# Reordering a software-pipelined two-layer graph attention kernel on TensorE: transposes of the next pair ahead of the scores, softmax rows transposed as a padded block, another order in prologue and drain

## What is computed

```python
def L0(X, adj, mask, Wqk, Wv):             # a softmax over the nodes
    q, k = split(X @ Wqk); v = X @ Wv
    agg = einsum('bij,bjd->bid', adj, k * mask)
    w = (1 / 16) * mask * einsum('bid,bid->bi', q, agg)
    return softmax(w, axis=1)[:, :, None] * v

def L1(x, adj, Wq, bq, Wk, bk, Wv, bv):    # dense attention, weighted by adj
    q, k, v = x @ Wq.T + bq, x @ Wk.T + bk, x @ Wv.T + bv
    weight = adj * exp(einsum('bqd,bkd->bqk', q, k))
    weight = weight / sum(weight, axis=2)
    return einsum('bqk,bkd->bqd', weight, v)

x = layernorm(x + L0(x, adj, ...)); x = layernorm(x + L1(x, adj, ...))
```

## Time and profile before

| | us |
|---|---|
| median of 3 runs | 321.32 |
| lowest, highest | 320.49, 321.69 |
| the profiled execution | 320.88 |
| its span, first to last instruction | 319.0 |
| TensorE busy | 303.7 (95%) |
| TensorE weight loads busy | 271.3 (85%) |
| VectorE busy | 221.3 (69%) |
| ScalarE busy | 200.4 (63%) |
| GpSimd busy | 141.7 (44%) |
| mean granted clock of TensorE | 0.993 of full |

### The profile page before, as it was taken

How to read it: one execution, slowest core, us unless ns; L and a number is a source line. 1 busy time by engine, 2 the same in 40 slices (tenths; PEclk the granted TensorE clock), 3 DMA queues, 4 the chain that set the end, 5 groups by cost and what they waited for, 6 DMA issues and landing times. The chain is left out here.

```text
span 319.0 us, 6523 instructions
## 1 busy us (share of the span) xinstructions
PE 303.7 (95%) x1898; PEld 271.3 (85%) x1898; DVE 221.3 (69%) x689; ACT 200.4 (63%) x456; POOL 141.7 (44%) x177
## 2 busy tenths in 40 slices
PE   8979999999999999999999999999999999999770
PEld 6758898889998988899989888999898889998660
DVE  1476777777767787777777877777778777767652
ACT  3445556667666666676666666766666667665562
POOL 1355553334555544345555344455553344553312
PEclk9999999999999999999999999999999999999997
DMA  7820223222333332323333332223333322110002
GB/s 247 296 66 36 82 85 115 86 82 84 100 115 115 115 114 83 82 87 94 115 115 115 115 87 78 83 98 115 115 115 115 91 73 82 66 53 34 33 35 99
DMA packets 19021, 31.26 MB, mean 98 GB/s; under 512 B 2112, under 2 KB 6336, under 8 KB 19008
## 3 DMA queue, kind: packets, MB, share of 16 engines
q1 hardware_dynamic: 19008, 31.11, 31.0%
HBM read 22.71 MB, written 8.39 MB: 97 GB/s over the span
## 5 line engine op out<-in xcount | busy, mean ns | idle before, releaser
L258 POOL TENSOR_TENSOR rstd<-var_eps,minus_half 128x4 f32<-128x4 f32 x35 | 35.6, 1017 | 157.6 <-ACT x L315 86.0
L315 ACT ACTIVATE x<-x_sum,shift,rstd 128x256 f32<-128x256 f32 x64 | 35.0, 594 | 48.6 <-POOL shift L261 48.6
L522 PE MATMUL ps<-w_hi,xt_hi 128*128 128x512 f32 x128 | 61.6, 482 | 0.4 <-DVE w_lo L511 0.3
L524 PE MATMUL ps<-w_hi,xt_lo 128*128 128x512 f32 x128 | 50.3, 393 | 0.0
L523 PE MATMUL ps<-w_lo,xt_hi 128*128 128x512 f32 x128 | 50.2, 392 | 0.0
L282 POOL TENSOR_TENSOR x1b<-x,bv_all 128x512 f32<-128x512 f32 x32 | 41.3, 1289 | 2.4 <-ACT x L315 2.4
L266 POOL TENSOR_TENSOR xt_lo<-xt_raw,xt_hi 128x512 fp32r<-128x512 f32 x31 | 40.0, 1290 | 4.8 <-ACT xt_hi L309 4.8
L522 PE MATMUL ps<-wv_hi,x1t_hi 128*128 128x258 f32 x128 | 38.9, 304 | 0.0
L362 ACT ACTIVATE z<-ps,z_bias 128x256 f32<-128x256 f32 x64 | 26.8, 470 | 16.3 <-PE ps L524 16.3
L315 ACT ACTIVATE x<-x,shift,rstd 128x256 f32<-128x256 f32 x64 | 34.9, 594 | 3.2 <-POOL shift L261 3.2
L394 DVE CUSTOM_DVE_ANT_0 agg<-ps,agg,adjt 128x256 f32<-128x256 f32 x64 | 31.0, 484 | 8.3 <-issue 5.7
(11 more groups left out here) (77 smaller groups left out, 646.0 us busy)
## 6 DMA issues: line engine op xcount, KB each, us to landing
xt_raw<-xt_pairs SPq DMA_DIRECT2D x32, 256.0 KB, 2.8
x_raw<-x_pairs SPq DMA_DIRECT2D x32, 256.0 KB, 2.7
out_pairs<-x SPq DMA_DIRECT2D x32, 256.0 KB, 2.0
adjt<-adjt_pairs SPq DMA_DIRECT2D x32, 129.0 KB, 2.1
p<-params SPq DMA_DIRECT2D x1, 770.0 KB, 6.8
p<-params SPq DMA_DIRECT2D x1, 512.0 KB, 3.8
p<-params SPq DMA_DIRECT2D x1, 256.0 KB, 4.8
bv_all<-value_bias SPq DMA_DIRECT2D x1, 128.0 KB, 7.5
```

Source lines behind the costliest of these rows:

```text
L258: nc.gpsimd.tensor_tensor(rstd[r % 2][:, :, :], var_eps[:, :, :], minus_half[:, :, :], ALU.pow)\
L315: last = nc.scalar.activation(out[:, graph(g)], in_[:, graph(g)], ACT.Identity, bias=shift[r % 2][:, layer, g:g + 1], scale=rstd[r % 2][:, ...
L522: nc.tensor.matmul(out, s_hi, m_hi, start=first, stop=False)
L524: return nc.tensor.matmul(out, s_lo, m_hi, start=False, stop=last)
```

## The change

- The x1 transposes become `transpose_x1(u, r)` and stand for pair t+1 between the values and the scores of slot t, instead of for pair t at the head of slot t. The copy `x1t` gets two buffers, and ScalarE makes it ahead of the exponentials.
- `p_row` becomes 128x128, zero but for its first two rows, and is transposed as a whole block.
- Prologue: the warm-up reads the zeroed `p_row`, has eight products and does not wait for `ident`; the second half of `m0` is split last; the projection of pair 0 is cut in halves with the aggregation after the first; pair 2 is masked, and aggregated, ahead of slot 0; `wv_lo` moves from slot -2 to slot -1 on GpSimd.
- Drain: in slot 30 ScalarE makes z before the norm of x1 of pair 31; in slot 31 TensorE does z before attend, and VectorE splits x1t first; the last output norm is made by VectorE in two halves, from `neg_mean` and `rstd`, and each half has its own store.

The diff, cut to its core:

```diff
...
-WARM_UP = 7
+WARM_UP = 8
...
-p_row = sb("p_row", [2, 128])
+p_row = sb("p_row", [128, 128])
...
-x1t = sb("x1t", [128, HALVES, 2, 128])
+x1t = [sb(f"x1t{i}", [128, HALVES, 2, 128]) for i in range(2)]
...
+p_row_zeroed = sem("p_row_zeroed")
...
-x1_done, out_done = sem("x1_done"), sem("out_done")
+x1_done, out_done, last_out_done = sem("x1_done"), sem("out_done"), sem("last_out_done")
...
 def w_row_ps(r):
...
+def p_full_ps(r):
+    return yv_ps(r)[:, 1, 0:NODES]
 def p_col_ps(r):
-    return yv_ps(r)[:, 1, 0:2]
+    return p_full_ps(r)[:, 0:2]
...
 def norms(t):
...
-        if exists(t - 3):
+        if r == LAST:
+            for g in range(2):
+                sp.wait_ge(last_out_done, g + 1)
+                sp.dma_start(out_pairs[t - 3][:, graph(g)], x2[(r - 3) % 4][:, graph(g)])\
+                    .then_inc(out_stored[(r - 3) % 4], 16)
+        elif exists(t - 3):
...
-    for q in out_stored:
-        sp.wait_ge(q, 16 + 16 * PAIRS // 4)
+    for n, q in enumerate(out_stored):
+        sp.wait_ge(q, 16 + 16 * PAIRS // 4 + 16 * (n == (PAIRS - 1) % 4))
...
 def _(pool):
...
-            mask_adj(t + 3, r + 3)
+            mask_adj(1, 1)
+            mask_adj(2, 2)
+        if r == -1:
...
-        if exists(t + 3) and r != -2:
+        if exists(t + 3) and r >= 0:
...
+    nc.gpsimd.memset(p_row[:, :], 0.0).then_inc(p_row_zeroed, 1)
...
+    def bias_z(t, r):
+        act.wait_ge(z_done, t + 1)
+        if r == 0:
+            act.wait_ge(biases_ready, 1)
+        for m in range(HALVES):
+            last = nc.scalar.activation(z[:, m, :], z_ps[:, m, :], ACT.Identity, bias=z_bias[:, m:m + 1])
+        last.then_inc(z_copied, 1)
     def slot(t, r):
+        if exists(t):
+            act.wait_ge(x1t_done, t + 1)
+            if exists(t - 2):
+                act.wait_ge(score_done, t - 1)
+            nc.scalar.copy(x1t[r % 2][:, :, :, :], x1t_ps).then_inc(x1t_copied, 1)
...
-        if exists(t):
-            act.wait_ge(x1t_done, t + 1)
-            nc.scalar.copy(x1t[:, :, :, :], x1t_ps).then_inc(x1t_copied, 1)
...
-        if exists(t - 3):
+        if exists(t - 3) and r != LAST:
...
+        if r == PAIRS - 2:
+            bias_z(t, r)
...
-        if exists(t):
-            act.wait_ge(z_done, t + 1)
-            if r == 0:
-                act.wait_ge(biases_ready, 1)
-            for m in range(HALVES):
-                last = nc.scalar.activation(z[:, m, :], z_ps[:, m, :], ACT.Identity, bias=z_bias[:, m:m + 1])
-            last.then_inc(z_copied, 1)
+        if exists(t) and r != PAIRS - 2:
+            bias_z(t, r)
...
+    act.wait_ge(m0_done, 1)
+    nc.scalar.activation(w0_hi[:, 0, 0:DIM], m0_ps[:, 0, :], ACT.Copy, scale=ATT_SCALE).then_inc(m0_hi_done, 1)
+    act.wait_ge(wv0_loaded, 16)
...
-        act.wait_ge(m0_done, m + 1)
-        nc.scalar.activation(w0_hi[:, m, 0:DIM], m0_ps[:, m, :], ACT.Copy, scale=ATT_SCALE).then_inc(m0_hi_done, 1)
-        act.wait_ge(wv0_loaded, 16)
...
+    act.wait_ge(m0_done, HALVES)
+    nc.scalar.activation(w0_hi[:, 1, 0:DIM], m0_ps[:, 1, :], ACT.Copy, scale=ATT_SCALE).then_inc(m0_hi_done, 1)
...
-    def split_x1t(t):
+    def split_x1t(t, r):
...
-        nc.vector.tensor_copy(x1t_hi[:, :, :, :], x1t[:, :, :, :]).then_inc(x1t_hi_done, 1)
+        nc.vector.tensor_copy(x1t_hi[:, :, :, :], x1t[r % 2][:, :, :, :]).then_inc(x1t_hi_done, 1)
...
-        nc.vector.tensor_tensor(x1t_lo[:, :, :, :], x1t[:, :, :, :], x1t_hi[:, :, :, :].bitcast(F32),
+        nc.vector.tensor_tensor(x1t_lo[:, :, :, :], x1t[r % 2][:, :, :, :], x1t_hi[:, :, :, :].bitcast(F32),
...
     def slot(t, r):
-        if r == 0:
-            split_x1t(t)
+        if r in (0, PAIRS - 1):
+            split_x1t(t, r)
...
-        if exists(t) and r != 0:
-            split_x1t(t)
+        if exists(t) and r not in (0, PAIRS - 1):
+            split_x1t(t, r)
...
-            nc.vector.tensor_scalar(p_row[:, :], exp_row[:, :], inv_sum[:, 0:1], None, ALU.mult)\
+            nc.vector.tensor_scalar(p_row[0:2, :], exp_row[:, :], inv_sum[:, 0:1], None, ALU.mult)\
...
+        if r == LAST:
+            dve.wait_ge(rstd_done, norms(t) - 1)
+            for g in range(2):
+                c = x2[(r - 3) % 4][:, graph(g)]
+                nc.vector.tensor_scalar(c, c, neg_mean[:, 1, g:g + 1], rstd[(r - 1) % 2][:, 1, g:g + 1],
+                                        ALU.add, ALU.mult).then_inc(last_out_done, 1)
...
-    for m in range(HALVES):
+    def low_m0(m):
...
+    low_m0(0)
+    for m in range(HALVES):
...
+    low_m0(1)
...
+    dve.wait_ge(consts_ready, 1)
...
+    def project_half(u, r, g, k):
+        if r == 0:
+            pe.wait_ge(m0_lo_done, k + 1)
+            pe.wait_ge(wv0_lo_done, k + 1)
+        return split_half(yv_ps(r)[:, g, :], xt_hi[r % 2][:, k, g, :], xt_lo[r % 2][:, k, g, :],
+                          w0_hi[:, k, :], w0_lo[:, k, :], k == 0, k == HALVES - 1)
     def project(u, r, g):
...
-        if r == 0:
-            pe.wait_ge(first_xt_lo_done, 1)
-        elif g == 0:
+        if g == 0:
...
-            if r == 0:
-                pe.wait_ge(m0_lo_done, k + 1)
-                pe.wait_ge(wv0_lo_done, k + 1)
-            mm = split_half(yv_ps(r)[:, g, :], xt_hi[r % 2][:, k, g, :], xt_lo[r % 2][:, k, g, :],
-                            w0_hi[:, k, :], w0_lo[:, k, :], k == 0, k == HALVES - 1)
+            mm = project_half(u, r, g, k)
...
     def transpose_w(u, r):
...
-        nc.tensor.transpose(p_col_ps(r), p_row[:, :], ident[0:2, 0:2]).then_inc(p_col_done, 1)
+        nc.tensor.transpose(p_full_ps(r), p_row[:, :], ident[:, :]).then_inc(p_col_done, 1)
...
     def fold_scores(m):
...
+    def transpose_x1(u, r):
+        pe.wait_ge(x1_done, u + 1)
+        if exists(u - 1):
+            pe.wait_ge(z_copied, u)
+        else:
+            pe.wait_ge(biases_ready, 1)
+        for g in range(2):
+            for k in range(HALVES):
+                c = g * DIM + k * 128
+                mm = nc.tensor.transpose(x1t_ps[:, k, g, :], x1[r % 2][:, c:c + 128], ident[:, :])
+        mm.then_inc(x1t_done, 1)
+    def attend(u):
+        pe.wait_ge(edge_done, u + 1)
+        pe.wait_ge(val_copied, u + 1)
+        for g in range(2):
+            mm = nc.tensor.matmul(sum_ps[:, g, 0:VAL_COLS], edge[:, graph(g, NODES)], val[:, g, :],
+                                  start=True, stop=True)
+        mm.then_inc(sum_done, 1)
     def slot(t, r):
-        if exists(t):
-            pe.wait_ge(x1_done, t + 1)
-            if exists(t - 1):
-                pe.wait_ge(z_copied, t)
-            else:
-                pe.wait_ge(biases_ready, 1)
-            for g in range(2):
-                for k in range(HALVES):
-                    c = g * DIM + k * 128
-                    mm = nc.tensor.transpose(x1t_ps[:, k, g, :], x1[r % 2][:, c:c + 128], ident[:, :])
-            mm.then_inc(x1t_done, 1)
-        if exists(t + 2):
-            aggregate(t + 2, r + 2)
+        if exists(t + 2):
+            if r > 0:
+                aggregate(t + 2, r + 2)
+            project(t + 2, r + 2, 0)
...
-        if exists(t + 2):
-            project(t + 2, r + 2, 0)
-        if exists(t - 1):
-            pe.wait_ge(edge_done, t)
-            pe.wait_ge(val_copied, t)
-            for g in range(2):
-                mm = nc.tensor.matmul(sum_ps[:, g, 0:VAL_COLS], edge[:, graph(g, NODES)], val[:, g, :],
-                                      start=True, stop=True)
-            mm.then_inc(sum_done, 1)
+        if exists(t - 1) and r != PAIRS - 1:
+            attend(t - 1)
...
+        if r == PAIRS - 1:
+            attend(t - 1)
...
+        if exists(t + 1) and exists(t):
+            transpose_x1(t + 1, r + 1)
+        if exists(t):
...
-                    mm = nc.tensor.matmul(score_ps[:, g, :], z[:, k, graph(g, NODES)], x1t[:, k, g, :],
+                    mm = nc.tensor.matmul(score_ps[:, g, :], z[:, k, graph(g, NODES)], x1t[r % 2][:, k, g, :],
...
-    pe.wait_ge(ident_ready, 1)
+    pe.wait_ge(p_row_zeroed, 1)
...
-        nc.tensor.matmul(ps[:, 0, 0:128], ident[:, :], ident[:, :], start=True, stop=True)
+        nc.tensor.matmul(ps[:, 0, 0:128], p_row[:, :], p_row[:, :], start=True, stop=True)
...
-    project(0, 0, 0)
+    pe.wait_ge(first_xt_lo_done, 1)
+    project_half(0, 0, 0, 0)
...
-    project(0, 0, 1)
+    project_half(0, 0, 0, 1).then_inc(yv_done[0], 1)
+    project_half(0, 0, 1, 0)
+    project_half(0, 0, 1, 1).then_inc(yv_done[1], 1)
...
+    aggregate(2, 2)
...
+    transpose_x1(0, 0)
...
```

## The result

The changed kernel takes 322.52 us (median of 17 runs, 322.04 to 322.79) against 321.02 for the kernel before (17 runs, 320.13 to 322.0): a ratio of 1.0042, 95% interval 1.0032 to 1.0052. It is slower by 1.5 us, less than the 0.5% that the prediction called no change, but clear of zero. Forecast were 322.0, within 317.6 to 324.6, and "within 0.5%" as the likeliest.

What follows compares the result with a forecast made beforehand. The prediction took TensorE's own sequence, 9.11 us a step, as the bound. Loop +2.3, prologue -0.45 and drain -1.2 gave +0.65 us, 322.0 against the median 321.32; range 317.6 to 324.6.

Steps and rivals of the forecast that it cites:

- The padded block: Softmax-row transpose in every loop step: as a full block it costs 0.11 instead of 0.30, saving 0.19 us a step.
- The moved transposes: Every step: x1 transposes ahead of the scores cost 0 themselves but uncover project's wait for graph 0's x_sum, ready at 1.06.
- The price of the wait: Every step, project's second matmul comes later through the wait for x_sum: 0.22 to 0.31 us lost, 0.27 taken.
- the prediction's second count: Last score matmul to project's second matmul, plus four moved transposes: 2.03 against 1.94 us now, +0.09 a step.
- Rival 3: Wait for graph 0's x_sum before project at upper price 0.31: +0.12 a step, +3.5, ends -1.2, 323.6 us; chance 0.2.
- What is late next: Other loop waits stay free; the w columns, free by little, would be the next bound at about 9.0 us a step.
- Prologue: Before the loop: fold_scores and p(0) 0.58 us sooner, p(2) at about 30.2 instead of 30.66: -0.45, bounds -1.5 and -0.1.
- the held cast: Prologue: VectorE's x1t_hi runs beside GpSimd's wv1_lo and x1b, and was let end near 22.7 us as before.
- Drain: After the loop: earlier x1t(31) and z(31), last norm on VectorE -0.75, split store 0: sum -1.2 us (-0.8 to -1.6).
- The rival in which the restart is hidden: Loop: TensorE's load runs on once x_sum is there, -0.05 a step, -1.5, ends -1.65: 318.2 us; chance 0.2.
- the one in which the padding does nothing: Loop: the full-block softmax transpose saves nothing, 2.11 against 1.94, +0.17 a step, +4.9: 324.6 us; chance 0.1.
- the fourth: Both small waits vanish and the ends give their most; no step under 9.0, -3.2 and -3.1: 315.0 us; chance 0.05.

## Why the prediction was right, point by point

**The padded block.** Right, with both its sizes: 0.11 from the last score matmul and 0.11 on, 0.19 less a step. It rested on the x1 transposes as the row of the same form. In the old order it is 0.16 by the steps (9.11 to 8.95) of the 0.19. The Trainium skill, page TensorEngine Tiling (Array Packing), section Tiling Modes, says that changing the tiling mode drains the array. These gaps going away agrees with it, but the experiments show only that the gaps belong to the small block, not by which mechanism: the padding takes the rows of the block and the columns that stream through it from 2 to 128 together, and no run parts the two.

**The moved transposes.** Right in the mechanism: an edit that moves work of equal cost took the cover from a dependency that no list of waits had shown, since it had 0.32 to spare. The chain was forecast at 1.06 and took 1.05. The dose (graph 1 first), the cover (the block between the scores) and the move alone show it, each within 0.02 of its forecast step.

**The price of the wait.** This is the term that was mis-sized: 0.27 taken, 0.30 measured (1.51 from block to second matmul against 1.21). With the prediction's second count, which had +0.09 a step where the first had +0.08, that makes the measured +0.12, and over 29 steps +3.5 instead of +2.3. Of the two rows that bounded it, that of the same instruction behind two waits was the true one (0.46 from data to second matmul in both), and I had gone halfway to the other. The exchanged waits show why: with the late wait last ahead of project's weight load the load follows 0.12 after the data, with the late one first 0.06. As recorded idle time the wait shows only 0.06 to 0.07 a step (1.9 us in 29), less than the 0.1 to 0.3 that was to be its sign. Rival 3 had this price, and the 0.30 stands at the mark from which the prediction would have it decide.

**What is late next.** Right that nothing was in the changed kernel, and too cautious where it named 9.0 us as the least: three kernels run at 8.94 and 8.95.

**Prologue.** p(0) was forecast 0.58 sooner and p(2) 0.45; the profile has 0.54 (15.59 to 15.05) and 0.26. The nearness at p(0) is in part luck. The 0.58 was the hole between the two halves of project, with the second at 9.31, and that hole belongs to one execution. The kernel before, then that of the moved transposes alone, whose prologue up to p(0) is the same; project's first matmul, and in the second also that of its second half:

```profile
8.03 0.47 PE L522 MATMUL ps<-w_hi,xt_hi 128*128 128x512 f32 x1
```
```profile
7.43 0.47 PE L524 MATMUL ps<-w_hi,xt_hi 128*128 128x512 f32 x1 [0.82 <-DVE w_lo L513]
...
8.20 0.45 PE L524 MATMUL ps<-w_hi,xt_hi 128*128 128x512 f32 x1
```

From the first to the second half it is 1.28 in the one and 0.77 in the other, so there is next to nothing for the aggregation to fill. From project's start to p(0) the changed kernel takes 6.90, the moved transposes alone 7.06 and the padded block alone, with the old prologue too, 6.90; only the kernel before takes 7.56. What the new order of the prologue is worth up to p(0) is therefore open, between 0 and 0.7. Behind p(0) the changed kernel takes 0.28 more to p(2) (15.35 against 15.07), forecast 0.13: the held cast, which ends 7.82 after p(0), 7.13 before and 7.69 in the forecast. That GpSimd's operation holds it is shown.

**Drain.** -1.27 against -1.2. z(31) started 8.99 after the softmax transpose of pair 31 (307.17 - 298.18), forecast 9.1; the scores of 31 12.9 after it, as forecast. The last norm took 0.77 after rstd, forecast 0.65, and the split of the store gave about 0.2 where I had put 0, so the nearness of the sum is in part two small misses that cancel.

**Sum.** In the profiled executions the span grew by 2.0 us (3.5 - 0.26 - 1.27), forecast 0.65, in the medians 1.5. Of the 1.35 between the profiles and the forecast 1.2 lie in the loop and 0.2 in the prologue, and the drain gave 0.07 more. So the direction and the mechanism were right, but the change came out over twice as large as forecast, and that 322.52 lies so near 322.0 is partly luck: the kernel before stood at 321.32 when the forecast was made and at 321.02 in the comparison. Rival 3 is the forecast's mechanism at the upper price: its +3.5 in the loop was exact, its ends (-1.2) fell short of the -1.53 measured, and its sum of +2.3 is nearer the 2.0 of the profiles than the forecast's. The rival in which the restart is hidden is out by the rows (0.46 from data to second matmul); the one in which the padding does nothing by the padded block alone; the fourth, in which no wait is left, by the step.

## What to carry to other kernels

When work of equal cost is moved along a saturated engine, ask which dependency it stood in front of, and measure that chain in the profile before: its slack is written in the starts, not in the list of waits. A transpose of two rows cost more here than one of a full block that is zero but for these rows (0.30 against 0.11 us), but what the padding saves counts only where nothing else is late. A TensorE that the profile calls busy throughout may still wait in each step: compare the distances of the starts. If a cheap operation starts a chain through another engine and back, put it early enough that the first engine has its own work until the chain returns, here into the middle of the scores.

## What the runs showed of the hardware that was not expected

The products of `m0` in the prologue, eight matmuls of 128x256, run at very different pace from one execution to the next, while the granted clock stands at 1.00, the 2.4 GHz level, in that stretch. The rows grouped by line, of the kernel before, of the changed one, and of the one with the last norm on ScalarE, whose instructions up to there are the changed kernel's:

```profile
L663 PE MATMUL ps<-p 128*128 128x256 f32 x8 | 3.3, 585 | 0.0
```
```profile
L705 PE MATMUL ps<-p 128*128 128x256 f32 x8 | 3.0, 544 | 0.0
```
```profile
L693 PE MATMUL ps<-p 128*128 128x256 f32 x8 | 2.0, 392 | 0.1
```

The stretch from 4 to 8 us of the last two, in the same order (the third number from the end is the granted clock):

```profile
4.00:8.00 4.00, 3.74 (x12) 2.70 (x11) 1.45 (x4) 1.79 (x5) 0.66 (x1) 1.00 1.01 341
```
```profile
4.00:8.00 4.00, 3.15 (x15) 2.23 (x14) 2.18 (x5) 1.96 (x5) 0.81 (x1) 1.00 0.97 321
```

The pace changes within an execution too. Of the changed kernel, the second and third of the eight products, and the last:

```profile
5.30 0.63 PE L705 MATMUL ps<-p 128*128 128x256 f32 x1
...
5.73 0.63 PE L705 MATMUL ps<-p 128*128 128x256 f32 x1
...
7.37 0.38 PE L705 MATMUL ps<-p 128*128 128x256 f32 x1
```

At first they follow each other by 0.43, the last three by 0.22: a factor of two, of which the recorded clock shows nothing. In the kernel before 0.43 holds up to the seventh, in the run with the last norm on ScalarE 0.22 from the second on. Whether the clock was in fact at its lower level is not shown. The products thus take between 2.0 and 3.3 us, and p(0) lies between 14.33 and 15.05 in the profiles of the eight kernels that have the changed kernel's start. Differences of half a microsecond between single profiles of this kernel, the prologue's among them, should be read from a later event to another, not from the start of the span.

That the place of a late wait among two, with the same instructions behind it, is worth 0.06 up to project's weight load, 0.04 a step, was not expected either.
